# A hybrid attention and feed-forward kernel: joined value products, roots by exp and ln, and a causal mask added by VectorE in all three score banks

## The reference, cut to what matters

```python
A1 = where(causal, Q1 @ K1.T * scaling, -inf)       # 16 heads, Dh = 8
A2 = where(causal, Q2 @ K2.T * scaling, -inf)       # so 32 maps of 256 x 256 a sequence
attn = softmax(A1) - lam * softmax(A2)
O = attn @ V
rms = sqrt(mean(O * O, axis=-1) + 1e-5)             # over the 16 columns of one head
O = O / rms * rms_scale * (1 - LAMBDA_INIT)
x = x + O @ Wo
```

## Time and profile before

| | us |
|---|---|
| three runs | 477.57, 476.18, 477.03 |
| profiled execution, its own time | 479.59 |
| its span, first to last instruction | 477.4 |
| first block (projections, weights) | 0 to 102.7 |
| attention with scores | 103.6 to 315 |
| attention without scores, and first feed-forward | 315 to 377 |
| linear attention | 370 to 447 |
| second feed-forward | 441 to 477 |

### The profile page before, as it was taken

The page is one execution under the profiler, slowest core; times in us unless marked ns, Lnnn a source line. Parts: engine busy times, 40 slices in busy tenths (PEclk is TensorE's granted clock), DMA queues, the critical chain, the costliest instruction groups (busy, mean ns, idle before and its releaser), DMA issues.

```text
span 477.4 us, 10025 instructions
## 1 busy us (share of the span) xinstructions
PE 414.0 (87%) x3380; PEld 267.7 (56%) x3380; DVE 316.5 (66%) x1139; ACT 261.0 (55%) x608; POOL 222.2 (47%) x332
## 2 busy tenths in 40 slices
PE   1666879978999989998998999896989899999996
PEld 0554635964655555555555555543567666655674
DVE  6575331249888979889897988934144499999311
ACT  2523310211677767676675767778757753354742
POOL 9433310035545647475454747556300577865100
PEclk9988779995899999999999999999899999999999
DMA  8589999907445455544145540000000000000011
GB/s 211 144 252 319 270 268 224 121 2 100 61 56 69 60 67 71 69 62 62 30 56 68 69 69 3 3 3 2 0 2 0 1 0 3 0 1 1 0 45 44
DMA packets 45041, 34.48 MB, mean 72 GB/s; under 512 B 19264, under 2 KB 40896, under 8 KB 43456
## 3 DMA queue, kind: packets, MB, share of 16 engines
q1 hardware_dynamic: 44992, 33.86, 37.4%
HBM read 25.20 MB, written 8.39 MB: 70 GB/s over the span
## 4 chain that ended last, share of the span: by engine, by line
PE 44%; DVE 11%; ACT 9%; issue 8%; POOL 4%; DMA 1%; DVEq 0%; SPq 0%; POOLq 0%; ACTq 0%
PE ps L1005 7%; PE ps L1049 6%; PE ps L1222 5%; PE ps L1026 5%; PE ps L1053 4%; DVE arena L1356 3%; PE ps L1030 2%; PE ps L1008 2%; PE ps L1213 2%; DVE arena L1369 2%; PE ps L1000 2%; PE ps L1126 2%; PE ps L1425 2%; PE ps L1096 2%; ACT arena L806 2%
## 5 line engine op out<-in xcount | busy, mean ns | idle before, releaser
L806 ACT ACTIVATE arena<-ps 128x512 f32<-128x512 f32 x192 | 115.0, 607 | 57.2 <-PE ps L1026 34.7
L758 POOL TENSOR_SCALAR_AFFINE_SELECT arena<-arena 128x256 f32<-128x256 f32 (+1 forms) x192 | 91.2, 485 | 92.8 <-ACT arena L806 91.0
L953 DVE TENSOR_REDUCE arena<-ps 128x2 f32<-128x512 f32 x128 | 85.9, 683 | 8.4 <-PE ps L1008 8.2
L948 DVE CUSTOM_DVE_ANT_0 ps<-ps,future 128x128 f32<-128x128 f32 x256 | 66.4, 320 | 10.8 <-PE ps L1000 9.1
L1297 POOL TENSOR_TENSOR arena<-arena 128x1024 f32<-128x1024 f32 x16 | 34.2, 2137 | 27.8 <-DVE arena L1382 27.3
L1049 PE MATMUL ps<-arena 128*17 128x256 f32 x512 | 40.1, 385 | 0.0
L1008 PE MATMUL ps<-future_bf,ident_bf 128*128 128x256 bf16 x128 | 37.0, 289 | 0.0
L1425 PE MATMUL ps<-arena,upto 128*128 128x384 f32 x96 | 36.0, 487 | 0.3 <-DVE arena L1356 0.3
L948 DVE DVE_READ_ACCUMULATOR2_ANT arena<- 128x1 f32 x256 | 35.6, 139 | 0.0
L388 POOL TENSOR_TENSOR qk_parts_sb<-qk_rest,qk_parts_sb 128x512 bf16<-128x512 f32 x16 | 19.1, 1211 | 30.6 <-DVE qk_parts_sb L492 30.6
L1222 PE MATMUL ps<-w,arena 128*128 128x128 f32 x256 | 30.3, 276 | 1.7 <-ACT arena L1189 1.2
(11 more groups left out here) (148 smaller groups left out, 836.8 us busy)
## 6 DMA issues: line engine op xcount, KB each, us to landing
qk_parts<-qk_parts_sb SPq DMA_DIRECT2D x16, 384.0 KB, 4.2
stack<-qk_parts SPq DMA_DIRECT2D x24, 256.0 KB, 6.8
arena<-qk_parts SPq DMA_DIRECT2D x24, 256.0 KB, 6.8
arena<-in_L_ffn_fc_B_dram SPq DMA_DIRECT2D x4, 1024.0 KB, 7.5
arena<-in_L_ffn_fc_A_dram SPq DMA_DIRECT2D x16, 256.0 KB, 5.0
xs<-in_L_attn_a_X_dram SPq DMA_DIRECT2D x4, 256.0 KB, 4.0
qk_parts<-qk_parts_sb SPq DMA_DIRECT2D x8, 128.0 KB, 4.7
out_dram<-xs SPq DMA_DIRECT2D x4, 256.0 KB, 2.3
```

The source lines that it names most:

```text
L758: nc.gpsimd.affine_select(out=diag, in_=diag, compare_op=ALU.is_ge, fill=0.0, base=0, pattern=[[0, 2 if s < 2 else UMAPS], [1, P]], channe ...
L806: nc.scalar.activation(probs[:, r, s, :], ps[:, bank, :], ACT.Exp, scale=SCALE).then_inc(exp_done, 1)
L948: last = nc.vector.tensor_tensor_reduce(out=block, in0=block, in1=future[:], scale=1.0, scalar=LOWEST, op0=ALU.add, op1=ALU.max, accum_out ...
L953: last = nc.vector.tensor_reduce(out=rowmax[:, gs, 1, at:at + 2], in_=ps[:, bank, :].rearrange("p (m k) -> p m k", m=2), axis=AX, op=ALU.max)
```

## The change

Three things change.

1. The mask of banks 1 and 2. The third matmul of a bank goes, with its bf16 constants; VectorE adds a mask of 256 columns (128 of zeros, 128 of the triangle) in two `tensor_tensor_reduce` a bank, in place of one `tensor_reduce`.
2. The value product: both halves of `weigh_values` are issued together behind bank 1.
3. Every inverse root is `exp(-0.5 * ln(x + eps))` on ScalarE, from one table that holds both functions. `root_step` goes; the squares are scaled by 0.25 before they are squared, so that their sum over 16 is the mean. The lags of the scaling, the transposes, the projection and the statistics fall by one.

```diff
-L_DEN, L_DIFF, L_SQ, L_MS, L_NORM, L_OPT, L_OPROJ, L_STAT = 16, 17, 19, 19, 22, 22, 23, 23
+L_DEN, L_DIFF, L_SQ, L_MS, L_ROOT, L_NORM, L_OPT, L_OPROJ, L_STAT = 16, 17, 19, 19, 20, 21, 21, 22, 22
+        def load_log_exp(act):
+            nc.scalar.preload_act_table_set("natural_log_exp_and_others")
...
@@ ScalarE, first block
-                load_table(act, ACT.Sqrt)
+                load_log_exp(act)
...
-                    nc.scalar.activation(std[:, c], moments[:, c, 1], ACT.Sqrt, bias=eps[:, 0:1]).then_inc(std_done, 1)
-                load_table(act, ACT.Exp)
+                    nc.scalar.activation(log_var[:, c], moments[:, c, 1], ACT.Ln, bias=eps[:, 0:1]).then_inc(log_done, 1)
+                    act.wait_ge(log_done, i + 1)
+                    nc.scalar.activation(rstd[:, c], log_var[:, c], ACT.Exp, scale=-0.5).then_inc(rstd_done, 1)
@@ ScalarE, attention: called behind the first exponential of a slot, after squares(it, j)
+            def inverse_root(it, j):
+                b = seq(it, j, L_ROOT)
+                if (j - L_ROOT) % UPS == 0 and live(b, SEQS):
+                    act.wait_ge(ms_raw, FIRST + b + 1)
+                    nc.scalar.activation(msum, msum, ACT.Ln, bias=eps[:, 0:1]).then_inc(ms_log, 1)
+                    act.wait_ge(ms_log, b + 1)
+                    if past(b):
+                        act.wait_ge(normed, FIRST + b)
+                    nc.scalar.activation(mrms, msum, ACT.Exp, scale=-0.5).then_inc(root, 1)
@@ VectorE, banks 1 and 2; root_step and its calls go
-                            last = nc.vector.tensor_reduce(
-                                out=rowmax[:, gs, 1, at:at + 2], in_=ps[:, bank, :].rearrange("p (m k) -> p m k", m=2),
-                                axis=AX, op=ALU.max)
+                            carry_wait(dve, tick_dve)
+                            for m in range(2):
+                                block = ps[:, bank, m * SEQ:(m + 1) * SEQ]
+                                last = nc.vector.tensor_tensor_reduce(
+                                    out=block, in0=block, in1=future_wide[:].rearrange("p a b -> p (a b)"), scale=1.0,
+                                    scalar=LOWEST, op0=ALU.add, op1=ALU.max,
+                                    accum_out=rowmax[:, gs, 1, at + m:at + m + 1])
@@ TensorE, banks 1 and 2
-                    nc.tensor.matmul(bank.rearrange("p (m k) -> p m k", m=2)[:, :, P:SEQ], ident_bf[:],
-                                     future_bf[:], start=False, stop=True,
-                                     skip_group_check=True).then_inc(scored, 1)
@@ TensorE, slot
-                    if s < TPS and live(unit(it, j, L_PV), UNITS):
-                        weigh_values(it, j, s)
+                    if s == 1 and live(unit(it, j, L_PV), UNITS):
+                        for t in range(TPS):
+                            weigh_values(it, j, t)
@@ ScalarE, between the slots of the attention (TAIL = 9; TAIL_OUT falls from 14 to 13)
                     if slot == TAIL - 3:
                         act.wait_ge(mom2_done, FIRST + 2 * SPB * 3)
-                        block_std(act, F1, 0, 1, 2)
+                        block_log(act, F1, 0, 1, 2)
+                        block_rstd(act, F1, 0, 1, 2)
...
                     if slot == TAIL + 1:
                         feed_gelu_scalar(act, F1, 0)
+                        load_log_exp(act)
                     if slot == TAIL_OUT:
+                        load_table(act, ACT.Gelu_apprx_tanh)
                         feed_rows_scalar(act, F1, 2)
```

More of the change, by code:

```diff
@@ L948, in emit @@
                                 last = nc.vector.tensor_tensor_reduce(
-                                    out=block, in0=block, in1=future[:], scale=1.0, scalar=LOWEST, op0=ALU.add,
+                                    out=block, in0=block, in1=future, scale=1.0, scalar=LOWEST, op0=ALU.add,
                                     op1=ALU.max, accum_out=rowmax[:, gs, 0, at:at + 1])
@@ L966, in emit @@
                     mean_squares(it, j)
-                    for s in range(BANKS_U):
-                        root_step(it, j, s)
                 b = seq(it, j, L_DEN)
@@ L1004, in score_bank @@
                     for m in range(2):
[L1005 to L1010 removed]
+                        last = nc.tensor.matmul(bank[:, m * SEQ:(m + 1) * SEQ], q[0:SROWS, m0 + 2 * s - 2 + m, P:SEQ],
+                                                k[0:SROWS, m0 + 2 * s - 2 + m, :], start=True, stop=True)
+                    last.then_inc(scored, 1)
             def shifted_bank(it, j, s):
@@ L1143, in feed_sems, with block_log, block_rstd, block_shift @@
         def feed_sems(tag):
-            return {k: sem(f"{tag}_{k}") for k in "std rstd ln xn xT xnT up gelu down res st mom stored".split()}
+            return {k: sem(f"{tag}_{k}") for k in "log rstd ln xn xT xnT up gelu down res st mom stored".split()}
         F1, F2 = feed_sems("f1"), feed_sems("f2")
-        def block_std(act, S, *blocks):
+        def block_log(act, S, *blocks):
             for k in blocks:
                 c = slice(BT * k, BT * k + BT)
-                nc.scalar.activation(std[:, c], moments[:, c, 1], ACT.Sqrt, bias=eps[:, 0:1]).then_inc(S["std"], 1)
-        def block_rstd(dve, S, *blocks):
+                nc.scalar.activation(log_var[:, c], moments[:, c, 1], ACT.Ln, bias=eps[:, 0:1]).then_inc(S["log"], 1)
+        def block_rstd(act, S, *blocks):
             for k in blocks:
                 c = slice(BT * k, BT * k + BT)
-                dve.wait_ge(S["std"], k + 1)
-                nc.vector.reciprocal(rstd[:, c], std[:, c]).then_inc(S["rstd"], 1)
+                act.wait_ge(S["log"], k + 1)
+                nc.scalar.activation(rstd[:, c], log_var[:, c], ACT.Exp, scale=-0.5).then_inc(S["rstd"], 1)
+        def block_shift(dve, S, *blocks):
+            for k in blocks:
+                c = slice(BT * k, BT * k + BT)
                 dve.wait_ge(S["rstd"], k + 1)
```

122 lines of the change are left out of this document (38 added, 84 removed).

## The result

The changed kernel takes 473.73 us (median of 10 runs, 472.18 to 475.03) against 477.23 for the kernel before on the same chip: a ratio of 0.9919 (of the means), interval 0.99 to 0.9939. The forecast was 462.0, its range 454 to 475. The direction was right and the time lies at the range's upper end, but -3.5 is under a quarter of the -15 forecast. The profiled executions differ by more, 477.4 to 471.9 in span: the one of before lay 2.4 us above its median, the one of after 0.2.

What follows compares the result with a forecast made beforehand. TensorE bounds plain slots now, VectorE close behind and bounding after the change. -1.0 + 1.3 - 0.8 - 3.7 - 15.0 + 4.0 - 0.4 = -15.6, less 0.6 given back: -15.0 from 477.03, so 462.0 us, range 454 to 475.

Steps and rivals of the forecast that it cites:

- The price of a 256-column map: VectorE's masked maxima: 0.38 us per 256-column instruction, between 0.30 and 0.50; four of them add 0.33 a slot.
- The work that TensorE sheds in a plain slot: Mask matmul gone, -0.22 us, and value products joined, -0.23: a plain slot falls from 2.88 to 2.43.
- the opening's slot: Slots before any exponential, bound by VectorE: 2.15 us becomes 2.48, four slots costing +1.3.
- the first sequence: First attention sequence, 24.69 us before: VectorE's 8 x 2.48 and two shifts make about 21.0, so -3.7.
- VectorE's side: VectorE's work a sequence: root steps take off 3.7 us, maps add 8 x 0.33, so 24.0 becomes 23.0.
- the sum of a sequence: VectorE's 23.0 us of work plus 2.2 of waits: 25.2, bound by VectorE; six sequences give -15.0.
- flat allowance for waits: VectorE's own waits in a sequence: 2.2 us, between 1.3 and 3.7, against 3.7 before.
- second rival: Engines hold one another in the sequences: waits stay 3.7 and the shift's way shows; 471 us (468 to 476), 18%.
- TensorE's side: TensorE's time for a sequence with the shed work: from 27.69 to about 24.1 us if nothing else held it.
- behind the last units: Work after the last attention units: two losses, together +4.0 us (0 to +6).
- Both losses named: First: rows of block 0 start later behind statistics, +1.3 us; second: ScalarE's rows of block 2 come later, +2.7.
- the clock as a rival: TensorE stands more and its granted clock falls to 0.5 in some stretches of a sequence: 482 us, 3%.

Runs made afterwards that it cites:

- R: Kernel before with only the inverse roots by ln and exp and their lags changed, mask and value products as before: 481.56 us.
- J: Kernel before with only the value products of both blocks joined: 469.61 us.
- J, R: Changed kernel with only its mask put back on TensorE (joined value products, roots by ln and exp): 471.07 us.
- J, M: Kernel before with joined value products and the mask on VectorE, root steps still there: 476.09 us.
- the two kernels with equal work for VectorE: Changed kernel with TensorE adding the mask again in one unit of each group of four: the last unit, 469.35 us, or the second, 470.63 us.
- the two edits of the rows: Changed kernel with ScalarE's rows of block 2 a slot earlier, 470.14 us; with statistics' shift and rows of blocks 0 and 1 also a slot earlier, 468.95 us.
- M: Kernel before with only the mask of the second and third bank moved to VectorE's maxima, root steps kept: 484.68 us.

## Why the prediction was wrong

**Right.** The price of a 256-column map is 0.38, where the rule of the Trainium skill that the forecast weighed (Vector Engine (DVE) Microarchitecture Reference, section Points that are easy to get wrong) would have made it 0.52; by that rule, the trace disagrees for an instruction with one of its sources in PSUM. The work that TensorE sheds in a plain slot came out too (2.43, measured 2.44), and so did the opening's slot (2.48, measured 2.52) and the first sequence (21.0, measured 21.4). `Ln` and `Exp` are hidden in a sequence, at 0.31 and 0.23 us:

```profile
L846 ACT ACTIVATE arena<-arena,eps 128x32 f32<-128x32 f32 x1 | 0.3, 306 | 0.0
L850 ACT ACTIVATE arena<-arena 128x32 f32<-128x32 f32 x1 | 0.2, 231 | 0.0
```

At the start the table load of the earlier trace rows is gone, and a copy stands where it was.

```profile
12.25 0.30 ACT L402 ACTIVATE log_var<-moments,eps 128x4 f32<-128x4 f32 x1 [0.64 <-DVE moments L456]
12.58 0.20 ACT L404 ACTIVATE rstd<-log_var 128x4 f32<-128x4 f32 x1
12.69 0.63 ACT L409 COPY xnT<-ps 128x256 f32<-128x256 f32 x2
```

**Wrong: "VectorE's side", the sum of a sequence, 25.2.** Two terms were short. The work is 23.70, not 23.0. Root steps took 2.0 to 2.2 and not 3.7, by the busy time of VectorE in a typical sequence of the three pairs that differ in R: 24.02 to 21.83 (before and R), 23.34 to 21.26 (J and J, R), 25.64 to 23.70 (J, M and after). I had added up durations from the trace. They overlap with their neighbours, and one can hold a wait: the step of line 917 takes 640 ns before and 228 in J. (They are also 13 instructions, not 11, one of them the mean of the squares.) Joining takes 0.7 of busy time off VectorE with the same instructions, and the mask adds 2.4 to 2.6, the forecast's 8 x 0.33. From before over J and J, R to the change: 24.02 - 0.68 - 2.08 + 2.44 = 23.70. And the waits are 26.57 - 23.70 = 2.9, not 2.2. Together that is 1.4 a sequence. The six miss their forecast by 7.7 us and not 8.3, as a sequence before takes 27.80 on average and not the 27.7 of the one looked at.

That is the arithmetic; the step behind it is the one to learn from. I set 23.0 beside 24.1 and let the larger bound every slot, with a flat allowance for waits. In fact TensorE still bounds the plain slots (2.44), VectorE's lag is carried through them, and TensorE stands for it at the transposes of the maxima, twice a sequence: 2.1 us where it had stood 1.1 before and stands 1.1 with no mask at all. The prediction counted two long slots of eight. There are three: 27.69 - 4.68 - 4.79 leaves 18.22 for the other six, not 6 x 2.88 = 17.28, and the third, 3.81, is a slot with these transposes. The earlier trace rows showed a plain slot, where nobody waits; I never looked at the one place where TensorE wants maxima that are not a unit old. No mask at all, the two kernels with equal work for VectorE and the one with the transposes moved show that this place has its own price. In the second rival ("the engines hold one another") the range, 468 to 476, holds the result, but its mechanism was the shift's transfer. In the six sequences no run shows TensorE waiting for that transfer more than before.

**Wrong: "TensorE's side", 24.1.** With VectorE relieved a sequence is 24.96. I had taken the shed work off every slot in full, and not every slot gives it. Against a typical sequence before, less 0.45 a slot, the kernel with no mask has 0.3 more in the reciprocal's slot, 0.1 in the first slot with the shift, and 0.4 in the slots with scaling, projection and the second shift, where TensorE still stands 1.1 for GpSimd. Of the 1.84 forecast for joining, 27.61 - 26.10 = 1.5 came (R against J, R); of TensorE's mask, 1.14 of 1.76 (J, R against no mask).

**Too small: behind the last units, +4.0 less 0.4, measured +5.9.** Both losses named are there, R alone makes them, and the two edits of the rows take them away. The changed kernel's timeline, to set beside the earlier trace rows:

```profile
322.64 0.42 DVE L892 TENSOR_TENSOR xs<-ps,xs 128x256 f32<-128x256 f32 x1 [9.15 <-PE ps L1093]
324.57 3.18 ACT L1138 ACTIVATE arena<-xs,shift_ln,rstd 128x128 f32<-128x128 f32 x8
336.57 0.32 ACT L846 ACTIVATE arena<-arena,eps 128x32 f32<-128x32 f32 x1 [0.75 <-DVE arena L901]
337.17 1.28 ACT L213 ACT_TABLE_LOAD   x1
338.57 1.63 ACT L1138 ACTIVATE arena<-xs,shift_ln,rstd 128x128 f32<-128x128 f32 x4
340.26 0.66 PE L1177 MATMUL ps<-ident,arena 128*128 128x128 f32 x4 [4.35 <-ACT arena L1138]
```

Counted from the last sequence's end (315.59 before, 304.20 after), rows of block 0 start 20.4 us on instead of 18.3: +2.1, forecast +1.3. TensorE's transposes of block 2 come at 36.1 instead of 31.7: +4.4, forecast 4.0. TensorE stands 4.35 us there instead of 1.50. So the first loss was 2.1 and not 1.3, the second 2.3 and not 2.7. What I had not priced comes next: TensorE's granted clock falls behind this stand, from 1.00 (2.4 GHz) to 0.50 (1.2 GHz). The stretches before and after it:

```profile
334.30:340.26 5.96, 1.61 (x5) 0.39 (x3) 0.69 (x1) 4.37 (x11) 1.91 (x2) 1.00 0.00 0
340.26:342.00 1.74, 1.74 (x11) 1.74 (x12) 0.00 (x0) 1.74 (x4) 0.00 (x0) 0.69 0.04 9
342.00:344.00 2.00, 2.00 (x12) 2.00 (x10) 0.00 (x0) 0.60 (x2) 0.00 (x0) 0.50 0.00 0
```

The 32 products behind it took 5.36 us. Before, behind the stand of 1.50, the clock was 1.00 and they took 3.74. With the rows of block 2 early TensorE waits 0.21 there, the clock stays at 1.00 and they take 3.74 again, so 1.6 us is the clock's:

```profile
336.39 0.66 PE L1177 MATMUL ps<-ident,arena 128*128 128x128 f32 x4 [0.21 <-ACT arena L1138]
336.89 3.74 PE L1194 MATMUL ps<-w,arena 128*128 128x128 f32 x32
```

2.1 + 2.3 + 1.6 is the 5.9, within 0.1. The two edits bear it out: block 2's rows early take away 4.0 (2.3 + 1.6), those of blocks 0 and 1 another 1.9 (the 2.1). The forecast had the clock as a rival for the sequences, and not for the one long stand that it forecast itself. In the changed kernel's sequences it stayed at 1.00; with the mask's move alone it did fall there.

**Left open.** What the mask's move costs is small against the spread. The medians say 2.7, 1.4 and 2.2 us (plain, block 2's rows early, all rows early), the ratios 1.7, 1.4 and 1.7, the profiles' sequences 1.4; I take about 1.5. The first value product of the kernels starts anywhere from 120.6 to 124.5 us; that no edit orders this makes me take it for chance of single executions, but nothing was run on it. Why M's sequences have the clock's spells and those of J, M, with stands as long, have none isn't shown either.

## What to carry to other kernels

When work moves between two engines that are close in load, don't compare their sums: list the places where one asks the other for something fresh, and move no work into the last piece before such a place. The same mask cost about 1.5 us everywhere and gained about 5 where three units of eight kept it on TensorE. Take an engine's work from its busy time in a stretch, not from durations added up. And a shared table for ln and exp is only free where no third function comes between: there, do all that needs no new value before the late root.

## What the hardware showed that was not expected

Not every stand of TensorE costs it its clock. In the changed kernel's sequences stands of 1.1 to 1.2 us left it at 1.00. Behind the 4.35 us it fell, and the products cost 1.6 us more. With the mask's move alone a stand of 1.82 us comes in five of the six sequences. Behind four of them the clock fell to 0.50 within 1.5 us, behind one it didn't; a fifth fall came 1.5 us behind a stand of 1.62. With J and M together stands of up to 1.92 us were followed by none.

In the changed kernel it was also at 0.50 where the attention runs out. TensorE had been busy 0.66 of 2.30 us ahead of the next-to-last projection, which then took 2.08 us instead of the 1.16 that it takes in a sequence. Before, the same projection took 1.83 us at a mean clock of 0.58, so this isn't the change's.

```profile
320.52:322.60 2.08, 2.08 (x12) 1.85 (x16) 0.00 (x0) 0.80 (x6) 0.00 (x0) 0.50 0.00 0
318.20:320.50 2.30, 0.66 (x4) 0.42 (x4) 0.00 (x0) 1.16 (x5) 1.52 (x2) 0.99 0.00 0
```

And a `tensor_tensor_reduce` takes 0.13 us for 128 more columns (0.25 to 0.38), the slope of a plain two-operand instruction on PSUM.
